# Keys turned off TensorE, key projections moved ahead of the queries', and three small pieces moved to ScalarE

## What is computed

```python
Q = (x @ Wq.T).reshape(Bb, Tt, H, S)
K = (x @ Wk.T).reshape(Bb, Tt, H, S)
V = (x @ Wv.T).reshape(Bb, Tt, H, HD)
dl = (x @ Wdl.T).reshape(Bb, Tt, H, LV)
g = A[None, None, :] * softplus(x @ Wdt.T + dt_bias)
Lam = softplus(Lp[None, None] * dl)
cg = jnp.cumsum(g, axis=1)
decay = exp(where(tri, cg[:, :, None, :] - cg[:, None, :, :], NEG))
scores = einsum('bthd,bshd->bhts', Q, K) * S ** (-0.5)
Wmat = scores * decay * lam_ts          # lam_ts: Lam at the level of (t xor s)
Y = einsum('bhts,bshd->bthd', Wmat, V)
o = Y @ Wout.T + x
a = layernorm(o) * ln_g + ln_b
x = layernorm(x + a)
# then, over t of 2 steps: c = sigmoid(..f) * c + sigmoid(..i) * tanh(..c)
# h = tanh(x_t @ wo.T + c_final @ uo.T + bo);  x = layernorm(x + h)
```

## Time and profile before

| | |
|---|---|
| median of three runs | 671.96 us |
| the profiled execution | 675.62 us |
| its span in the profile | 674.0 us |
| TensorE busy | 656.2 us, 97% |
| VectorE busy | 486.4 us, 72% |
| ScalarE busy | 336.9 us, 50% |
| GpSimd busy | 354.1 us, 53% |
| mean busy share of the 16 DMA engines by q1, which holds SP's transfers | 26.6% |

### The profile page before, as it was taken

How to read it: one execution, slowest core, us unless ns; L and a number is a source line. 1 busy time by engine, 2 the same in 40 slices (tenths; PEclk the granted TensorE clock), 3 DMA queues, 4 the chain that set the end, 5 groups by cost and what they waited for, 6 DMA issues and landing times.

```text
span 674.0 us, 22147 instructions
## 1 busy us (share of the span) xinstructions
PE 656.2 (97%) x9114; PEld 594.3 (88%) x9114; DVE 486.4 (72%) x1100; ACT 336.9 (50%) x755; POOL 354.1 (53%) x475
## 2 busy tenths in 40 slices
PE   9989999999999999999999999999998999999994
PEld 7889999999999999899999999999987788888894
DVE  3864887779787978676887879787986656655556
ACT  5555454444545454555454445545552343555555
POOL 1806555646464646556554636474883335343425
PEclk9999999999999999999999999999997999999998
DMA  9123130414131222203140313122336403140002
GB/s 304 51 58 64 45 89 28 92 31 88 41 77 54 66 65 67 69 27 87 31 93 28 89 30 88 36 67 74 92 81 126 68 9 62 52 82 31 33 33 93
DMA packets 91987, 45.47 MB, mean 67 GB/s; under 512 B 39664, under 2 KB 90480, under 8 KB 91888
## 3 DMA queue, kind: packets, MB, share of 16 engines
q1 hardware_dynamic: 91888, 44.06, 26.6%
HBM read 34.60 MB, written 9.44 MB: 65 GB/s over the span
## 4 chain that ended last, share of the span: by engine, by line
PE 85%; DVE 6%; ACT 2%; POOL 2%; issue 2%; SPq 1%; DMA 0%; DVEq 0%; POOLq 0%
PE bank L436 64%; PE bank L460 5%; PE bank L439 4%; PE bank L527 4%; PE bank L492 4%; PE bank L556 4%; DVE t L1027 1%; ACT t L790 1%; SPq L347 1%; DVE t L1030 1%; ACT E L790 1%; SPq L370 1%; POOL t L1414 1%; DMA yT<-xscr 0%; POOL yL L1414 0%
## 5 line engine op out<-in xcount | busy, mean ns | idle before, releaser
L436 PE MATMUL bank<-xH,wH 128*128 128x256 f32 x480 | 144.4, 301 | 1.2 <-ACT KT L790 0.9
L436 PE MATMUL bank<-xL,wH 128*128 128x256 f32 x480 | 135.0, 281 | 0.0
L436 PE MATMUL bank<-xH,wL 128*128 128x256 f32 x480 | 134.5, 280 | 0.0
L1027 DVE TENSOR_TENSOR W<-bank,E 128x512 f32<-128x512 f32 x128 | 82.1, 685 | 23.9 <-PE bank L436 23.6
L436 PEld LDWEIGHTS bank<-xH,wH 128*128 128x128 f32 x480 | 90.4, 188 | 7.8 <-issue 7.3
L436 PEld LDWEIGHTS bank<-xL,wH 128*128 128x128 f32 x480 | 90.5, 189 | 0.4
L436 PEld LDWEIGHTS bank<-xH,wL 128*128 128x128 f32 x480 | 90.5, 188 | 0.0
L790 ACT ACTIVATE E<-bank 128x512 f32<-128x512 f32 x128 | 66.1, 602 | 46.8 <-PE bank L460 46.8
L790 ACT ACTIVATE QT<-bank 128x512 f32<-128x512 f32 x64 | 38.2, 597 | 98.5 <-PE bank L436 98.5
L436 PE MATMUL bank<-QT,KT 64*128 64x128 f32 x1024 | 66.3, 280 | 0.0
L436 PEld LDWEIGHTS bank<-QT,KT 64*128 64x128 f32 x1024 | 60.2, 189 | 4.8 <-issue 0.8
(11 more groups left out here) (151 smaller groups left out, 1650.5 us busy)
## 6 DMA issues: line engine op xcount, KB each, us to landing
cB<-scr SPq DMA_DIRECT2D x240, 64.0 KB, 3.0
xt<-in_xT SPq DMA_DIRECT2D x16, 256.0 KB, 2.8
xs<-in_x SPq DMA_DIRECT2D x16, 256.0 KB, 3.2
xscr<-tx SPq DMA_DIRECT2D x32, 128.0 KB, 2.8
yT<-xscr SPq DMA_DIRECT2D x64, 64.0 KB, 2.5
out<-xs SPq DMA_DIRECT2D x16, 256.0 KB, 2.1
xt<-in_wffn SPq DMA_DIRECT2D x8, 256.0 KB, 3.0
QT<-in_wqk SPq DMA_DIRECT2D x4, 256.0 KB, 5.8
```

Of the source, the lines that this page charges most:

```text
L436: return e.matmul(o, a, b, start=start, stop=stop)
L1027: return e.tensor_tensor(o, a, b, op)
```

## The change

The keys are no longer turned by TensorE. VectorE turns 32x32 blocks of `KT` (`turn_keys`), SP stores them in a new DRAM buffer `kscr`, and loads them back into `Kt` with the blocks in their places (`load_keys`: four transfers of 32 partitions, in runs of 32 numbers, 128 bytes). Each pair has four such turns and stores, each chunk one set of four loads. The first pair uses `W` as buffer, the others `kx`. The state update now waits for the landing of `Kt`.

The projection jobs of all pairs but the first go keys, keys, queries, queries, twice (`part`), so that the keys are there earlier. `outer_norm` goes from VectorE to ScalarE, as a scale and a shift, with one small product on GpSimd and a negation on ScalarE; the sum of the outer residual is written into `xs`, and `x1` is gone. `turn_result` and `store_turned` move by a step to distance 12, with one buffer `tx`. The copy `cgt` goes to ScalarE for all pairs but the first. SP's coefficient loads are split by chunk over two steps, the last FFN weight and the first `yT` come earlier, and the FFN weights stand in another order (`GX`, `GU`).

```diff
-SPLIT = [0, 4, 1, 5, 2, 6, 3, 7]
+SPLIT = [4, 5, 0, 1, 6, 7, 2, 3]
+def part(sg, j):
+    if sg == 0:
+        return j % 2 == 0, j - j % 2
+    return j % 4 >= 2, 4 * (j // 4) + 2 * (j % 2)
+def copied(sg, q):
+    return next(j for j in range(8) if part(sg, j) == (False, 2 * q)) + 1
+def key_jobs(s):
+    out = []
+    for d, q in ((7, 0), (5, 1), (3, 2), (2, 3)):
+        if (s + d) % 8 == 0 and 1 <= (s + d) // 8 < NSG:
+            out.append(((s + d) // 8, q))
+    return out
...
+            def store_keys(sg, q):
+                e.wait_ge(d_kx, 4 * sg + q + 1)
+                src, done = (kx[:, :], l_kx) if sg else (W[:, 4 * q:4 * q + 4, :].rearrange("p h t -> p (h t)"), l_k0)
+                e.dma_start(kscr[4 * sg:4 * sg + 4, :, 512 * q:512 * q + 512].rearrange("i t c -> (i t) c"),
+                            src).then_inc(done, 16)
+            def load_keys(ci):
+                sg, c = ci // 2, ci % 2
+                e.wait_ge(l_kx, 64 * sg) if sg else e.wait_ge(l_k0, 64)
+                if STATE[ci]:
+                    e.wait_ge(p_st, STATE[ci])
+                for j in range(4):
+                    b = 128 * c + 32 * j
+                    e.dma_start(Kt[32 * j:32 * j + 32, :].rearrange("t (q i f) -> t q i f", q=8, i=4),
+                                kscr[4 * sg:4 * sg + 4, :, :].rearrange("i t (q b) -> t q i b", q=8)[:, :, :, b:b + 32]
+                                ).then_inc(l_Kt, 16)
...
             for s in STEPS:
-                for i in [i for i in range(8) if s == (NG - 20 if i < 2 else NG - 17 + i)]:
+                for i in [i for i in range(8) if s == (NG - 20 if i < 2 else min(NG - 17 + i, NG - 10))]:
                     load_wf(i)
                 for sg, j in token_jobs(s):
                     if j == 5:
-                        load_coefs(sg)
-                        if sg + 2 < NSG:
-                            load_x(sg + 2)
+                        store_coefs(sg)
...
-                if s in (NG - 8, NG - 7):
-                    load_turned(0, s - NG + 8)
-                if (ci := chunk_at(s, 11)) is not None:
+                if (ci := chunk_at(s, 12)) is not None:
                     store_turned(ci)
+                for q in range(4) if s == -2 else ():
+                    store_keys(0, q)
+                for sg, q in key_jobs(s):
+                    store_keys(sg, q)
+                if 0 <= s < NG and s % 8 == 3 and s // 4 + 1 in STATE:
+                    load_keys(s // 4 + 1)
+                if -1 <= s < NG - 8 and s % 8 == 7:
+                    load_keys((s + 1) // 4)
+                if s == -1:
+                    load_coefs(0, 1)
...
+                if s in (NG - 10, NG - 7):
+                    load_turned(0, (s - NG + 10) // 3)
+                for sg, j in token_jobs(s):
+                    if j == 5:
+                        load_coefs(sg, 0)
+                for sg, j in token_jobs(s - 1):
+                    if j == 5:
+                        load_coefs(sg, 1)
+                        if sg + 2 < NSG:
+                            load_x(sg + 2)
...
-            def keys(ci):
-                c, b = ci % 2, (ci // 2) % 2
-                if c == 0:
-                    e.wait_ge(a_qk, 8 * (ci // 2) + 8)
-                for n in range(2):
-                    m, u = MISC["keys", ci, n]
-                    if u:
-                        e.wait_ge(m_free[m], u)
-                    for q in range(4):
-                        t = tr(MB[m][:, 128 * q:128 * q + 128], KT[b][:, 4 * n + q, 128 * c:128 * c + 128])
-                    t.then_inc(p_kt, 1)
...
-                km, ku = MISC["keys", ci, 0]
-                e.wait_ge(m_free[km], ku + 1)
-                km, ku = MISC["keys", ci, 1]
-                e.wait_ge(m_free[km], ku + 1)
+                e.wait_ge(l_Kt, 64 * (STATE[ci] + 1))
...
+                if j == 3 and sg:
+                    m, u = MISC["cgt", sg, 0]
+                    e.wait_ge(p_cg, sg + 1)
+                    e.wait_ge(d_ll, sg)
+                    e.wait_ge(g_at, 2 * sg)
+                    act(cgt[:, :], MB[m][:, 0:320], ACT.Copy).then_inc(m_free[m], 1)
...
-                    act(Kt[:, 512 * n:512 * n + 512], MB[m][:, :], ACT.Copy).then_inc(m_free[m], 1)
...
+            def outer_norm(ci):
+                e.wait_ge(g_rs2, ci + 1)
+                act(nb2[:, :], nm2[:, :], ACT.Copy, scale=-1.0).then_inc(a_n2, 1)
+                e.wait_ge(a_n2, ci + 1)
+                act(xs[:, ci, :], xs[:, ci, :], ACT.Identity, scale=rs2[:, 0:1], bias=nb2[:, 0:1]).then_inc(a_x2, 1)
...
+            def turn_keys(sg, q):
+                e.wait_ge(a_qk, 8 * sg + copied(sg, q))
+                src = KT[sg % 2][:, 2 * q:2 * q + 2, :].rearrange("p m t -> p (m t)")
+                if sg == 0:
+                    o = W[:, 4 * q:4 * q + 4, :].rearrange("p h t -> p (h t)")
+                else:
+                    o = kx[:, :]
+                    if sg > 1 or q:
+                        e.wait_ge(l_kx, 16 * (4 * (sg - 1) + q))
+                e.transpose(o, src).then_inc(d_kx, 1)
...
-                if (ci := chunk_at(s, 11)) is not None:
-                    outer_norm(ci)
+                if (ci := chunk_at(s, 12)) is not None:
                     turn_result(ci)
+                for sg, q in key_jobs(s):
+                    turn_keys(sg, q)
```

More of the change, by code:

```diff
@@ L29 @@
 B_END = 1200
-WF, WI, WC, UF, UI, UC, WO, UO = range(8)
+GX, GU, WO, UO = (4, 5, 0), (1, 6, 7), 2, 3
 def bc(ap, axis, n):
@@ L85, in misc_jobs @@
         ci, cc = s // 4, (s // 4) % CB
-        if s % 4 == 0 and cc < CB - 1:
-            out += [("keys", ci, 0), ("keys", ci, 1)]
         if s % 4 == 1 and cc:
@@ L171, in program @@
         xscr = nc.dram_tensor("xscr", (4 * NC, 32, 256), F32, kind="Internal").ap()
+        kscr = nc.dram_tensor("kscr", (4 * NSG, 32, 2048), F32, kind="Internal").ap()
         def sb(name, shape, dt=F32):
@@ L191, in program @@
         oo = sb("oo", [P, 256])
-        x1 = sb("x1", [P, 256])
-        tx = [sb(f"tx{i}", [P, 256]) for i in range(2)]
+        tx = sb("tx", [P, 256])
+        kx = sb("kx", [P, 512])
         st1 = sb("st1", [P, 6])
@@ L337, in load_coefs @@
                 e.dma_start(scr.rearrange("a l c t -> (a l) (c t)"), cT[:, :]).then_inc(l_sc, 16)
+            def load_coefs(sg, c):
                 e.wait_ge(l_sc, 16 * sg + 16)
[L339 to L348 removed]
+                ci = 2 * sg + c
+                if ci in INTER:
+                    if ci >= 2 and ci - 2 in INTER:
+                        for h in range(2):
+                            m, u = MISC["inter", ci - 2, h]
+                            e.wait_ge(m_free[m], u + 1)
+                    for a in range(8):
+                        e.dma_start(cB[c][16 * a:16 * a + 16, :, :, :].rearrange("p l u t -> p (l u) t"),
+                                    scr[a, :, c, :].partition_broadcast(16)).then_inc(l_cB[c], 16)
@@ L355, in load_turned @@
             def load_turned(blk, t):
                 c0 = 16 * t + 4 * blk
-                for i in range(2):
-                    e.wait_ge(l_tx[i], 16 * (c0 // 2 + 2))
+                e.wait_ge(l_tx, 16 * (c0 + 4))
                 if blk == 0:
@@ L592, in first_project @@
             def first_project(j):
-                q = j % 2 == 0
-                Q, m0 = banks[5 * (j % 2)], j if q else 8 + j - 1
+                q, m0 = part(0, j)
+                Q, m0 = banks[5 * (j % 2)], m0 if q else 8 + m0
                 if j < 4:
@@ L622, in project @@
             def project(sg, j):
-                b, Q, q = sg % 2, banks[project_bank(j)], j % 2 == 0
-                m0 = j if q else 8 + j - 1
+                b, Q = sg % 2, banks[project_bank(j)]
+                q, m0 = part(sg, j)
+                m0 = m0 if q else 8 + m0
                 e.wait_ge(g_xl, sg)
@@ L646, in first_bias @@
                 e.wait_ge(a_qk, 8 * NSG)
-                e.wait_ge(g_wf, SPLIT.index(UC) + 1)
+                e.wait_ge(g_wf, max(SPLIT.index(w) for w in GU) + 1)
                 e.wait_ge(g_c0, 1)
@@ L751, in _ @@
                 if 0 <= ci < NC:
-                    if n == 0 and ci in STATE:
-                        keys(ci)
                     if n == 1:
@@ L806, in project @@
                 n = 5 * (j % 2) if sg == 0 else project_bank(j)
-                b, q = sg % 2, j % 2 == 0
-                m0 = j if q else 8 + j - 1
+                b = sg % 2
+                q, m0 = part(sg, j)
                 src = banks[n][:, :].rearrange("p (m t) -> p m t", m=2)
@@ L877, in exps @@
                     act(E[:, :, 32 * q:32 * q + 32], XP[q][:, :].rearrange("p (h t) -> p h t", h=H), ACT.Exp).then_inc(a_e, 1)
-            def keys(ci):
-                for n in range(2):
-                    m, u = MISC["keys", ci, n]
-                    e.wait_ge(p_kt, 2 * STATE[ci] + n + 1)
-                    if ci - 1 in STATE and n == 0:
-                        e.wait_ge(p_st, STATE[ci - 1] + 1)
```

(10 more changed lines are left out.)

84 lines of the change are left out of this document (39 added, 45 removed).

## The result

The changed kernel takes 696.2 us (median of four runs, 692.65 to 705.21) against 672.1 for the kernel before in the same comparison: ratio 1.033, 95% interval 1.026 to 1.039. One of the four, 705.21, ran at a lower clock than the others (0.955 against 0.966 to 0.972) and is not in the ratio. The forecast was 657. The profiled run took 695.46 us (span 693.6), 19.8 more than the profiled run before, which at 675.62 was itself 3.7 us above its kernel's median. Its page first, with the rows that the edit was about; columns as in the earlier trace rows.

A forecast was written before the change was run, and what follows sets the result against it. TensorE was taken to bound the steady part. Pairs 1 to 14 gain 1.1 us each, 15.4, chunk 1 0.85, the tail -1: together 15 us off the median 672.0, giving 657 us, range 644 to 668.

The forecast's parts named there:

- What TensorE gives back: Steady part: dropping the transposes of keys frees 0.85 us of TensorE per chunk, 1.7 us a pair.
- VectorE's slack: Before the exponents: VectorE's added turns make TensorE late by 0.3 us in even chunks, 0.2 on average in odd ones.
- VectorE would be the bound: Rival, steady pairs: added turns delay waiting matmuls, leaving 0.3 to 0.6 us gain a pair, 665 us; chance 0.13.
- The keys' load, "late by 0.1": Before the even chunk's state update: last load lands at 326.5, TensorE wants it at 326.4; bounds 0 and 2 us.
- The tipping point: Even state update: a loss once the wait passes 1.4 us, with landing over 6.8 us after the first issue.
- the rival of the loads: Each pair waits for keys at the even state update: slower, 689 us at 8 us landing, 717 at 10; chance 0.09.
- The signs: In the profile after: state-update waits over 1 us would mean late loads; load issues over 1 us, a wrong forecast.
- The head: First chunk: keys land at 44.5 us, needed by 44.83; no net change, but chunk 0's 0.85 us is not gained.
- The tail: Before the gates: 5 us wait for the last keys, against the 2.62 us wait for `yT` going; -1 us taken.
- The fit of the Trainium skill: Loads of keys: 2.0 us plus bytes over 436 GB/s, 3.2 us for 0.5 MB, no late arrival; not used in the sum.

The follow-up runs named there:

- the half change: Kernel before with norm's end and decays' copy on ScalarE, only odd chunks' keys turned by VectorE and loaded, first store ahead of coefficient loads: 663.2 us, ratio 0.986.

## Why the prediction was wrong, step by step

- **What TensorE gives back**, 1.7 us a pair: right for one block (0.83 each in the half change), too much for both. With all blocks gone and nothing in their place a pair gains 1.47.
- **VectorE's slack**, 0.3 for the even chunk and 0.2 for the odd: right in size. `CT` waits 0.16 us in most pairs, and all of VectorE's added work costs 0.36 a pair (30.33 - 29.97), against the 0.5 in the sum. This miss and the one above go opposite ways and leave 1.1 where the sum has 1.2; that the two agree so well is in part luck. That VectorE would be the bound is excluded: with all its added work, the kernel without the keys' loads is 2.2% faster than before.
- **The keys' load, "late by 0.1": this is the step that failed.** In the pair shown the wait was 1.24 us and on average 1.41, and the low clock came behind it. From the end of the statistics, 351.33, SP's first issue of keys was 11.2 us later (10.5 forecast; the sixteen loads took 3.70 + 5.25 us where I had given 8.47), and the last landing another 6.2 (5.5 forecast). TensorE came when it was expected to, within 0.3. Two misses of 0.7 make 1.4 less 0.3; with the 0.1 it is about the 1.24 seen. Over the 14 pairs the landing took 6.1 to 7.6 us, 6.6 on average. The wrong part of it is the 2.1 us that I took over from `yT` as all that comes beyond the packets' own time. The packets themselves cost what I had said (12.9 ns each, 3.3 us of all engines), but by the trace the first of them starts 1.7 us after the first issue, they spread over 4.3 us, and 0.6 us pass from the last to the landing. One issue in four takes over 1 us (29 of 120). It was not that other transfers filled the engines: with the keys ahead of half of the coefficients, and for the odd chunks of the half change, the four loads take as long.
- **The tipping point** in the rival of the loads (loss from 6.8 us of landing, 1.4 of wait) lay just beyond the value taken. The measured landing averages 6.6 and the wait 1.41, so by that rule the pairs should come out even. They lose 0.84. The rival was the right one at a chance of 0.09, with the right place and a price that was still too low: its 689 us belonged to a wait of 2.6 us. Two things were missing. A pair had 1.1 us to lose and not 1.4 (the 0.2 for `CT` in the odd chunk is not in that rule), and
- **the clock was in no step.** 0.49 us a pair, 6.8 in the pairs, hang on the same wait: 1.10 - 1.41 - 0.49 = -0.80, against -0.84 measured. The prediction mentioned the clock only for the tail. The stretch that it named there, 511 to 518 us, does not come right behind a standstill of TensorE: in before the clock falls at 510.95, ten us after the wait for `CT`, amid the two-column matmuls of `first_bias`, with TensorE busy.

```profile
510.90 0.31 PE L436 MATMUL bank<-c0H,wH 128*128 128x2 f32 x1
```

- **The signs** that the prediction named: waits of state updates over 1 us, the mark of this rival, and issues of the keys' loads over 1 us, a sign of being wrong, both came. One load landed in 3.1 to 5.1 us, about as it said; it is the set of four that took longer.
- **The head**, "a wash": +3.0 us. 0.9 come from the weights' low half, wanted earlier; the wait for `ng` grew from 0.5 to 1.5 us, and a stretch of half clock follows it at 43.4. The kernel with long runs has both waits and not that stretch, and its exponents of chunk 1 start at 46.9 in place of 48.9, so the clock is the larger part. The keys of chunk 0 landed at 45.03, near the forecast 44.5, and nothing waited for them.
- **The tail**, -1: +6.0. The wait of about 5 us for the last keys is there (4.9), and none for `yL`, as forecast. Missed: 2.74 us for `CT` at 517.52, where 1.04 was, and the clock, at half speed for 20.5 us of this stretch (from 500.7, 517.8 and 528.1) against 6.8 before. Timelines of TensorE and SP at the tail of after:

```profile
517.52 1.86 PE L521 MATMUL bank<-CT,AT 32*128 32x128 f32 x32 [2.74 <-DVE CT L1317]
...
529.77 3.01 SPq L396 DMA_DIRECT2D Kt<-kscr  x4
```

The stretch up to the gates:

```profile
536.00:541.70 5.70, 5.63 (x96) 5.00 (x96) 1.62 (x4) 1.65 (x4) 0.72 (x1) 0.50 0.63 111
```

  13.65 us of that half clock begin at 528.1, before the last wait, and amid the two-column matmuls, as in before. The run without even loads, the one without transposes and the one with only the new order of projections have a stretch as long around their gates, so the keys are not its cause alone; what sets its length was not settled.
- **The fit of the Trainium skill** (DMA: Bandwidth & Descriptors, Anatomy of one DMA) against the row of `yT`: the row was nearer, but both were too kind. By the fit (2.0 us and bytes over 436 GB/s, 3.2 us for the 0.5 MB) nothing would have waited; measured were 6.1 to 7.6 with short runs, and 4.9 and more with runs of 1 KB. The fit is given for transfers that GpSimd issues, and these are SP's. The Trainium skill's rule on disjoint partitions was not tried: no run loads the keys with one transfer.

Summed up, by the ratios: the loads cost 37 us (1.033 - 0.978 of 672), and 34 of these are the even chunks' (1.033 - 0.982). The 3 us between are not in the pairs and are hardly more than the intervals. Of the 37, 20 go with the shortness of the runs. Moving eight coefficient loads and `x` behind the keys ends the steady waits for keys and saves 9 us (1.033 - 1.019), since late coefficients take their place. How the 37 divide between SP's order and the loads' own time stays open.

## What to carry to other kernels

Moving work off the bound engine through memory pays where the loop has a gap longer than the whole way, and not where the margin is tenths of a microsecond: count the whole way of a set of transfers from the first issue to the last landing (the issues, the start, the packets, the end), not one transfer's landing with the packets' time added, and take the longest and not the median, for it varied from 6.1 to 7.6 us between pairs that do the same work. Where two halves of a loop have different gaps (here 4.1 to 6.1 us and 11 to 15 us from the first issue to the use), move only the half whose gap is longer than the way. A repeated wait of TensorE of 1.4 us can cost more than 1.4 us, since the clock may fall behind it; here that added 0.49 us a pair to 1.41.

## What was not expected of the hardware

- A single wait of 1.4 to 2.4 us in an otherwise busy TensorE was followed in five places by 3.4 us at 1.2 GHz; others of 1.36 (at 337.49), 1.24 (at 368.79) and 1.17 us were not. Length alone does not decide it: with runs of 1 KB a wait of 1.82 us (at 107.03) was not followed by a lower clock, where 1.37 us was in after (at 400.58).
- The issue of one load of 1024 runs of 128 bytes took 0.56 to 2.01 us on SP, with a median of 0.70; with runs of 1 KB the median was 0.43. With one large broadcast load ahead, the third issue of four took 2.2 to 6.1 us before even chunks in the pairs, 4.6 as a median. The instructions of that line in after (count: shortest, median, longest in ns):

```profile
L396 SPq DMA_DIRECT2D Kt<-kscr x120: 562/704/2009, 38.4 to 531.8; - x120
```

and with one load of `cB`:

```profile
L395 SPq DMA_DIRECT2D Kt<-kscr x120: 562/686/6099, 38.3 to 565.6; - x120
```

- 0.5 MB by one broadcast load in place of eight removed 14 issues a pair and took the kernel from 1.033 to 1.071 of before, 25 us; the same edit on the kernel before changed it by 0.3%.
